# Local attention layers with a load semaphore each for the weights of queries and of keys

## The chip, the cores and the metric

The kernel runs on one core of one Trainium2 chip. The metric is the device time of one execution in microseconds (us), and the median of several runs stands for a kernel. PE is the tensor engine, DVE the vector engine, ACT the scalar engine, POOL GpSimd, and SP the engine whose queue issues the DMAs.

## The reference

Two blocks of gated cross attention and a feed-forward part, over an input of 32 sequences of 128 tokens with 128 features. The first "feed-forward" part is itself a stack of six local attention layers with an MLP each; nearly all of the time goes there, and the change touches nothing else.

```python
def attn_layer(x, Wqkv, qs, ksc, Wo):          # 16 heads of 64, windows of 32 tokens
    q, k, v = jnp.split(x @ Wqkv, 3, -1)       # each (b, heads, n, 64) after sh
    q = l2norm(q) * qs
    k = l2norm(k) * ksc
    q = q * cos * scale + rotate_half(q) * sin * scale
    k = k * cos * inv + rotate_half(k) * sin * inv
    out = local_attention(q, k, v)             # softmax over this window and the one before
    return out.transpose(0, 2, 1, 3).reshape(b, n, INNER) @ Wo

for i in range(6):
    x = attn_layer(shift_tokens(x), Wqkv[i], q_scale[i], k_scale[i], Wo[i]) + x
    x = ffn_layer(shift_tokens(x), ln_g[i], ln_b[i], W1[i], b1[i], W2[i], b2[i]) + x

x = x + jnp.tanh(g_xattn[0]) * cross_attention_0(layernorm(x), ctx)
x = x + jnp.tanh(g_ffn[0]) * local_layers(layernorm(x))
x = x + jnp.tanh(g_xattn[1]) * cross_attention_1(layernorm(x), ctx)
x = x + jnp.tanh(g_ffn[1]) * quantised_linear(layernorm(x))
```

## The kernel before

Activations stay in SBUF for the whole kernel. There are three phases: the first cross attention, `local_layers` with all six layers, and the second cross attention with the quantised linear. Between phases every engine drains.

In `local_layers` a unit u is one sequence of one layer, 6 x 32 = 192 units. Every engine runs the same loop over steps, and in a step it does a stage of several units at once: the projection of queries and keys of unit `step`, their transposes of unit `step - 1`, the scores of `step - 2`, the value projection of `step - 4`, the mix of `step - 6`, and the MLP of a group of four sequences between 7 and 13 steps behind. The order of the stages in a step is written out by hand for each engine; there is no scheduler. Engines wait for each other by semaphores with constant counts. The pipeline doesn't empty between layers: step 32 k is the first of a new layer, and in it PE still makes values, scores and MLP of the old one.

PE's order in a step is: queries (`project(step, 0)`), the MLP's third up projection (every fourth step, the first of a layer among them), `mix`, keys (`project(step, 1)`), values (`project(step - 4, 2)`), `scores`, the output projection (odd units), other parts of the MLP, and the transposes of keys and of queries. Each of these takes one of four pairs of PSUM banks in turn (`ROTATING`), and `banks.fill` waits for the reader of what the pair held four turns ago. At the first step of a layer the values take the pair of that step's queries, so PE waits there for `producted[0]`, which DVE raises on line 1027. The scores take the pair of the third up projection and wait for `hidden_made`, which DVE raises on line 1101.

Weights have one buffer each: queries, keys and values lie side by side in `w_qkv`, and the head scales `qs` and `ks` in `head_scales`. SP loads a part of the next layer when PE has made the last projection with it. In the last-but-one step of a layer, behind the copies of moved values (`place_v`), it issues the query weights and the query scales (`load_qk(sp, layer + 1, 0)`), and in the last step, behind the four DMAs that bring turned probabilities back (`place_probs`), the key weights and the key scales (`load_qk(sp, layer + 1, 1)`). Behind those stand the DMAs of `place_v` and the store of turned probabilities.

All four DMAs of a layer raise the common semaphore `qk_loaded`, which is at `QK * (layer + 1)` when the last has landed. Two waits use it: PE's before the first query projection of a layer, and DVE's in `start_layer`, which stands before all DVE's work of the step and makes `rot`, the rotary tables multiplied by the head scales. `start_layer` has four small products of two SBUF tiles (128x64 each): the two for queries on lines 1012 and 1014, then the two for keys on the same lines. Behind it DVE's order is: the query products with `rot` (lines 1026 and 1027, one operand in PSUM; they also wait for ACT's squares, line 896), the turning of probabilities (line 1074), the gelu product (line 1101), and the key products (lines 1026 and 1027 again).

ACT's order at the start of a step is: squares of the queries, the reciprocal norms of the unit before (line 907), one gelu, squares of the keys. POOL's is: rotation of the keys of the unit before (line 1154), their normalisation and that of its queries (both line 1162, which wait for line 907), subtraction of the row maxima (line 1140), rotation of the queries (line 1154), and normalisation of probabilities (line 1146). All POOL's operations have both inputs in SBUF.

Of the kernel before, what the change touches and what calls it, by code (L numbers as in the profile page):

```python
# [16 lines left out]
P = 128  # L17
NB, S, D = 32, 128, 128
# [9 lines left out]
INNER = H * HD  # L28
IT = INNER // P
FF = int(D * 4 * 2 / 3)  # L30
FTILES = [(o, min(P, FF - o)) for o in range(0, FF, P)]
# [33 lines left out]
def each(n):  # L65

    def of(stage):
        def run(u, *more):
            if 0 <= u < n:
                stage(u, *more)  # L70
        return run
    return of
# [46 lines left out]
def build(nc, dram):  # L119
    stack = ExitStack()  # L120
    with stack:
# [3 lines left out]
        def sem(name):  # L125
            return stack.enter_context(nc.semaphore(name))
# [426 lines left out]
        def local_layers(phase):  # L553
            here = ExitStack()
            with here:
# [28 lines left out]
                (gelu,) = ring("gelu", 1, [P, len(FTILES), GT])  # L584
                mlp_x2 = mlp_xs[:, :, :].rearrange("p b s -> p (b s)")

            qk_loaded, wv_loaded, wo_loaded, mlp_loaded = sem("qk_loaded"), sem("wv_loaded"), sem("wo_loaded"), sem("mlp_loaded")
            QK, WV, WO, MLP = 16 * 4, 16, 16, 16 * (1 + 3 * len(FTILES) + 3)
            zeroed, rot_made, xs_ready = sem("zeroed"), sem("rot_made"), sem("xs_ready")
            projected = [sem(f"projected_{k}") for k in "qkv"]  # L590
            v_copied, v_placed = sem("v_copied"), sem("v_placed")
# [1 line left out]
            squared, producted, summed, rotations, normalised, turned, copied = (  # L593
                [sem(f"{n}_{k}") for k in "qk"]
                for n in ("squared", "producted", "summed", "rotations", "normalised", "turned", "copied"))
# [17 lines left out]
            for step in range(UNITS + LAST):  # L613
                for stage, lag, every in ROTATING:
                    u = step - lag
# [9 lines left out]
            def load_qk(sp, layer, part):  # L625
                if layer:
                    sp.wait_ge(projected[part], NB * layer)
                sp.dma_start(w_qkv[:, part * INNER:(part + 1) * INNER],
                             dram["l_wqkv"][layer, :, part * INNER:(part + 1) * INNER]).then_inc(qk_loaded, 16)
                if layer:  # L630
                    sp.wait_ge(rot_made, 4 * layer)
                sp.dma_start(head_scales[:, part, :, :].rearrange("p s d -> p (s d)"),
                             dram[("l_qs", "l_ks")[part]][layer].partition_broadcast(P)).then_inc(qk_loaded, 16)

            def load_v(sp, layer):
                if layer:
# [54 lines left out]
            def load_first(sp):  # L691
                load_qk(sp, 0, 0)
                load_qk(sp, 0, 1)
                load_v(sp, 0)
                load_out(sp, 0)
                load_mlp(sp, 0)

            def sp(sp):
                for step in range(UNITS + LAST):
                    place_probs(step - 5, sp)  # L700
                    layer, into = step // NB, step % NB
                    if layer < DEPTH - 1 and into == NB - 1:
                        load_qk(sp, layer + 1, 1)
                    if 0 < layer < DEPTH and into == 3:
                        load_v(sp, layer)
                    place_v(step - 4, sp)
                    if layer < DEPTH - 1 and into == NB - 2:
                        load_qk(sp, layer + 1, 0)
                    if 0 < layer < DEPTH and into == 5:
                        load_out(sp, layer)  # L710
                    if 0 < layer < DEPTH and into == 12:
                        load_mlp(sp, layer)
                    store_probs(step - 4, sp)
                sp.wait_ge(probs_placed, P_PLACED * UNITS)

            def pe(pe):
# [3 lines left out]
                @each(UNITS)  # L720
                def project(u, part):
                    g = u // GB
                    i = pair_of["qkv"[part], u]
                    banks.fill(pe, i, (producted[part] if part < 2 else v_copied, u + 1))
                    if u % NB == 0 and part == 0:
                        pe.wait_ge(qk_loaded, QK * (u // NB + 1))
                    if u % NB == 0 and part == 2:
                        pe.wait_ge(wv_loaded, WV * (u // NB + 1))
                    if u % GB == 0 and part == 0:
                        pe.wait_ge(xs_ready, g + 1)  # L730
                    for j in range(2):
                        mm = pe.matmul(pairs[i][:, j * BANK:(j + 1) * BANK], xs[g % 2][:, u % GB, :],  # L732
                                       w_qkv[:, part * INNER + j * BANK:part * INNER + (j + 1) * BANK], start=True, stop=True)
                    mm.then_inc(projected[part], 1)
# [107 lines left out]
                for step in range(UNITS + LAST):  # L842
                    project(step, 0)
                    mlp_up(step - 13, 2)
                    mix(step - 6)
                    project(step, 1)
                    project(step - 4, 2)
                    scores(step - 2)
                    project_out(step - 6)
                    mlp_up(step - 11, 0)  # L850
                    mlp_mean(step - 7)
                    mlp_up(step - 11, 1)
                    mlp_variance(step - 10)
                    mlp_down(step - 13)
                    transpose_qk(step - 1, 1)
                    transpose_qk(step - 1, 0)
# [146 lines left out]
            def dve(dve):  # L1003
                phase_gate(dve, phase)

                def start_layer(layer):
                    dve.wait_ge(qk_loaded, QK * (layer + 1))
                    if layer:
                        dve.wait_ge(producted[0], NB * layer)
                        dve.wait_ge(producted[1], NB * layer)  # L1010
                    for i in range(2):
                        dve.tensor_tensor(rot[:, 2 * i, :, :], tables[:, 2 * i, :, :], head_scales[:, i, :, :],
                                          ALU.mult).then_inc(rot_made, 1)
                        dve.tensor_tensor(rot[:, 2 * i + 1, :, :], tables[:, 2 * i + 1, :, :], head_scales[:, i, ::-1, :],
                                          ALU.mult).then_inc(rot_made, 1)
# [96 lines left out]
                for step in range(UNITS + LAST):  # L1112
                    if step < UNITS and step % NB == 0:
                        start_layer(step // NB)
                    products(step, 0)
                    turn_probs(step - 5)
                    mlp_hidden(step - 13, 2)
                    products(step, 1)
                    mask_scores(step - 2)
                    sum_squares(step, 0)  # L1120
                    mlp_centre(step - 7)
                    add_out(step - 6)
                    mlp_hidden(step - 11, 0)
                    add_down(step - 13)
                    sum_squares(step, 1)
                    mlp_hidden(step - 11, 1)
                    row_sums(step - 4)
                    clamp_norms(step)
                    row_maxima(step - 2)
# [51 lines left out]
            return load_first, sp, pe, act, dve, pool  # L1181

        f0_load, f0_sp, f0_pe, f0_act, f0_dve, f0_pool = local_layers(1)

        def second_attention(phase):
# [714 lines left out]
```

## Time and profile before

| | |
|---|---|
| median of 3 runs | 3425.03 us (3424.27 to 3427.98) |
| the profiled execution's own time | 3413.21 us |
| its span | 3411.4 us |
| mean granted clock of PE | 0.982 of full speed |
| local layers in the span | from about 243 to 3060 us |
| busy over the span | PE 95%, DVE 86%, POOL 77%, ACT 70% |
| chain of work that ended last | PE 84%, issue 5%, POOL 4%, ACT 3%, DVE 3% |

The profile is of one execution, with times in us from the start of the span. A timeline row has the start, the time taken, engine, line of the kernel, operation and tiles, the count if equal operations are merged, and in brackets the idle time of the engine before it with what ended it. "issue" there means that nothing which the profile shows ended it; a wait for a semaphore that a DMA raised long before is not told apart from others by that. In the time that an operation took, what it stood still after its start is contained.

The page names the costliest groups: the projections on line 732 (1081.2 us busy on PE) are the first, POOL's rotations on line 1154 (908.7 us) the second. A step lasts some 14.5 us, so the 192 units take most of the span.

### The profile page before, as it was taken

The numbers are of one execution on the slowest core, as the hardware profiler recorded it, in microseconds if no ns is written. First come the engines' busy times: TensorE is split into PE (matmuls) and PEld (weight loads), VectorE is DVE, ScalarE is ACT, GpSimd is POOL, SyncE is SP. The second block draws the span as 40 slices with busy tenths as digits, with TensorE's granted clock in tenths as the row PEclk, the third lists the DMA queues.
The fourth block names the chain that finished last, engine by engine and source line by source line (L and its number), as shares of the span: only waits on it lengthen the run. The fifth ranks groups of instructions, "written<-read, shape, count | busy, mean of one in ns | idle before, by whom it ended". The sixth has DMA issues, their size and how long they took to land.

```text
span 3411.4 us, 130897 instructions
## 1 busy us (share of the span) xinstructions
PE 3245.9 (95%) x56355; PEld 2054.7 (60%) x56386; DVE 2943.4 (86%) x3343; ACT 2379.1 (70%) x4288; POOL 2639.8 (77%) x1408
## 2 busy tenths in 40 slices
PE   7977999999999999999999999999999999977996
PEld 4545666666666666666666666666666666643554
DVE  6869989889999999998989898898999999935887
ACT  6865677667676767676776776776767676746885
POOL 1229988888888888888888888888888888833576
PEclk9989999999999999999999999999999999988998
DMA  2002333443433344334433334343344333330000
GB/s 94 2 1 64 122 113 111 120 126 114 120 112 112 117 126 119 113 108 126 125 113 117 112 110 123 119 120 113 113 125 125 118 111 112 110 123 1 2 11 17
DMA packets 229188, 336.05 MB, mean 99 GB/s; under 512 B 39046, under 2 KB 151044, under 8 KB 228228
## 3 DMA queue, kind: packets, MB, share of 16 engines
q1 hardware_dynamic: 228612, 327.68, 31.7%
q8 instruction: 446, 7.31, 0.9%
q14 instruction: 130, 1.06, 0.1%
HBM read 124.14 MB, written 102.76 MB: 67 GB/s over the span
## 4 chain that ended last, share of the span: by engine, by line
PE 84%; issue 5%; POOL 4%; ACT 3%; DVE 3%; SPq 0%; DMA 0%; POOLq 0%; DVEq 0%; ACTq 0%
PE psum L732 29%; PE psum L800 10%; PE psum L742 9%; PE psum L786 8%; PE psum L759 8%; PE psum L827 7%; PE psum L838 4%; POOL f_rotated L1154 2%; ACT x_expo L1480 1%; PE psum L817 1%; PE psum L809 1%; ACT x_expo L391 1%; PE psum L1337 1%; PE psum L1347 1%; PE psum L309 1%
## 5 line engine op out<-in xcount | busy, mean ns | idle before, releaser
L732 PE MATMUL psum<-w_qkv,f_xs 128*128 128x512 f32 x2304 | 1081.2, 606 | 18.9 <-issue 14.2
L1154 POOL TENSOR_TENSOR f_rotated<-f_times_cos,f_times_sin 128x1024 f32<-128x1024 f32 x384 | 908.7, 2367 | 9.3 <-DVE f_times_sin L1027 9.3
L1162 POOL TENSOR_TENSOR f_rotated<-f_rotated,f_rnorm 128x1024 f32<-128x1024 f32 x384 | 722.6, 1903 | 38.2 <-ACT f_rnorm L907 11.9
L732 PEld LDWEIGHTS psum<-w_qkv,f_xs 128*128 128x128 f32 x2304 | 410.1, 191 | 402.4 <-issue 393.6
L896 ACT ACTIVATE f_squares<-psum 128x1024 f32<-128x1024 f32 x384 | 392.9, 1023 | 361.4 <-PE psum L732 356.4
L1146 POOL TENSOR_TENSOR f_probs<-f_probs,f_rowsum 128x1024 f32<-128x1024 f32 x192 | 365.2, 1902 | 329.1 <-DVE f_rowsum L1066 329.1
L1026 DVE TENSOR_TENSOR f_times_cos<-psum,rot 128x1024 f32<-128x1024 f32 x384 | 469.8, 1223 | 131.6 <-ACT f_squares L896 127.8
L914 ACT COPY f_qkT<-psum 128x1024 f32<-128x1024 f32 x384 | 369.9, 1013 | 210.8 <-PE psum L742 210.7
L1027 DVE TENSOR_TENSOR f_times_sin<-psum,rot 128x1024 f32<-128x1024 f32 x384 | 466.1, 1214 | 0.0
L1034 DVE TENSOR_REDUCE f_sumsq<-f_squares 128x16 f32<-128x1024 f32 x384 | 463.4, 1209 | 0.0
L742 PEld LDWEIGHTS psum<-consts,f_rotated 128*128 128x128 f32 x3072 | 348.5, 141 | 98.0 <-issue 89.2
L742 PE MATMUL psum<-consts,f_rotated 128*128 128x128 f32 x3072 | 371.1, 274 | 17.7 <-POOL f_rotated L1162 14.7
L1140 POOL TENSOR_TENSOR f_probs<-f_probs,f_negmax 128x1024 f32<-128x1024 f32 x192 | 365.2, 1902 | 0.0
L786 PEld LDWEIGHTS psum<-f_probsT,f_v 64*64 64x64 f32 x6144 | 262.9, 135 | 163.1 <-issue 163.1
L800 PE MATMUL psum<-f_outT,w_o 128*128 128x256 f32 x1536 | 358.6, 387 | 1.2 <-ACT f_outT L928 1.2
L759 PEld LDWEIGHTS psum<-f_qkT 64*32 64x32 f32 x24576 | 254.2, 105 | 146.9 <-issue 145.3
L786 PE MATMUL psum<-f_probsT,f_v 64*64 64x64 f32 (+1 forms) x6144 | 310.1, 228 | 15.8 <-issue 15.8
L800 PEld LDWEIGHTS psum<-f_outT,w_o 128*128 128x128 f32 x1536 | 285.1, 190 | 45.5 <-issue 1.8
L786 PE MATMUL psum<-f_probsT,f_v_moved 64*64 64x32 f32 (+1 forms) x12288 | 307.5, 217 | 0.0
L827 PE MATMUL psum<-f_xn,w 128*128 128x512 f32 (+1 forms) x576 | 281.2, 612 | 7.7 <-ACT f_xn L970 7.7
L759 PE MATMUL psum<-f_qkT 64*32 64x64 f32 x24576 | 285.4, 225 | 0.8 <-issue 0.8
L786 PEld LDWEIGHTS psum<-f_probsT,f_v_moved 64*64 64x64 f32 x12288 | 286.2, 136 | 0.0
(175 smaller groups left out, 5159.5 us busy)
## 6 DMA issues: line engine op xcount, KB each, us to landing
f_v_moved<-f_v SPq DMA_DIRECT2D x768, 128.0 KB, 2.8
turned_blocks<-w_qkv SPq DMA_DIRECT2D x192, 512.0 KB, 3.0
f_probsT<-turned_blocks SPq DMA_DIRECT2D x768, 128.0 KB, 2.8
w_qkv<-in_l_wqkv SPq DMA_DIRECT2D x18, 512.0 KB, 4.0
w_o<-in_l_wo SPq DMA_DIRECT2D x6, 512.0 KB, 4.6
w_qkv<-in_ctxT SPq DMA_DIRECT2D x1, 2048.0 KB, 8.7
out<-x_f_result SPq DMA_DIRECT2D x8, 256.0 KB, 2.2
w<-in_l_w SPq DMA_DIRECT2D x6, 341.0 KB
```

Of the source, the lines that this page charges most:

```text
L732: mm = pe.matmul(pairs[i][:, j * BANK:(j + 1) * BANK], xs[g % 2][:, u % GB, :], w_qkv[:, part * INNER + j * BANK:part * INNER + (j + 1) * ...
L742: tr = pe.transpose(pairs[i][:, t * S:(t + 1) * S], rotated[u % 2][:, part, 2 * t:2 * t + 2, :].rearrange("p h d -> p (h d)"), ident)
L759: mm = pe.matmul(pairs[i][these, at:at + NEAR], qkT[u % 2][rows, 0, t, these], qkT[u % 2][rows, 1, t, near], start=True, stop=True, tile_p ...
L786: mm = pe.matmul(pairs[i][cols, at + windows.start * WIN:at + windows.stop * WIN], values, probsT[u % 2][rows, windows, j, :], start=True, ...
L800: mm = pe.matmul(pairs[i][:, 0:GT // 2], w_o[:, t, :], outT[:, t, tokens], start=t == 0, stop=t == IT - 1)
L827: mm = pe.matmul(pairs[i][0:n, a * BANK:a * BANK + GT], w_1[:, a * FF + o:a * FF + o + n], xn[:, :], start=True, stop=True)
L896: act.activation(squares[part][:, :], pair("qk"[part], u), ACT.Square).then_inc(squared[part], 1)
L1026: dve.tensor_tensor(halves(times_cos[part][:, :]), halves(taken), table(0), ALU.mult)
L1027: dve.tensor_tensor(halves(times_sin[part][:, :]), halves(taken)[:, ::-1], table(1), ALU.mult).then_inc(producted[part], 1)
L1034: dve.tensor_reduce(sumsq[u % 2][:, part * H:(part + 1) * H], squares[part][:, :].rearrange("p (s h d) -> p h s d", s=2, h=H), axis=XY, op ...
L1154: pool.tensor_tensor(rotated[u % 2][:, part].rearrange("p h (s d) -> p s h d", s=2), halves(times_cos[part][:, :]), halves(times_sin[part] ...
L1162: pool.tensor_tensor(rt, rt, rnorm[u % 2][:, part * H:(part + 1) * H].unsqueeze(2).broadcast_to([P, H, HD]), ALU.mult).then_inc(normalised ...
```

## The change

The common semaphore is replaced by two, `q_loaded` and `k_loaded`, each raised by two DMAs per layer. PE waits for the first before its first query projection of a layer and for the second before its first key projection. In `start_layer` DVE waits for `q_loaded` and `producted[0]`, makes the two query products of `rot`, and then waits for `k_loaded` and `producted[1]` and makes those for keys. SP issues the same DMAs in the same order behind the same waits, and no instruction of PE, ACT, DVE or POOL is moved, added or left out, but for the waits.

```diff
-            qk_loaded, wv_loaded, wo_loaded, mlp_loaded = sem("qk_loaded"), sem("wv_loaded"), sem("wo_loaded"), sem("mlp_loaded")
-            QK, WV, WO, MLP = 16 * 4, 16, 16, 16 * (1 + 3 * len(FTILES) + 3)
+            q_and_k_loaded = [sem("q_loaded"), sem("k_loaded")]
+            wv_loaded, wo_loaded, mlp_loaded = sem("wv_loaded"), sem("wo_loaded"), sem("mlp_loaded")
+            QK, WV, WO, MLP = 16 * 2, 16, 16, 16 * (1 + 3 * len(FTILES) + 3)
...
                 sp.dma_start(w_qkv[:, part * INNER:(part + 1) * INNER],
-                             dram["l_wqkv"][layer, :, part * INNER:(part + 1) * INNER]).then_inc(qk_loaded, 16)
+                             dram["l_wqkv"][layer, :, part * INNER:(part + 1) * INNER]).then_inc(q_and_k_loaded[part], 16)
                 if layer:
                     sp.wait_ge(rot_made, 4 * layer)
                 sp.dma_start(head_scales[:, part, :, :].rearrange("p s d -> p (s d)"),
-                             dram[("l_qs", "l_ks")[part]][layer].partition_broadcast(P)).then_inc(qk_loaded, 16)
+                             dram[("l_qs", "l_ks")[part]][layer].partition_broadcast(P)).then_inc(q_and_k_loaded[part], 16)
...
                     banks.fill(pe, i, (producted[part] if part < 2 else v_copied, u + 1))
-                    if u % NB == 0 and part == 0:
-                        pe.wait_ge(qk_loaded, QK * (u // NB + 1))
+                    if u % NB == 0 and part < 2:
+                        pe.wait_ge(q_and_k_loaded[part], QK * (u // NB + 1))
...
                 def start_layer(layer):
-                    dve.wait_ge(qk_loaded, QK * (layer + 1))
-                    if layer:
-                        dve.wait_ge(producted[0], NB * layer)
-                        dve.wait_ge(producted[1], NB * layer)
                     for i in range(2):
+                        dve.wait_ge(q_and_k_loaded[i], QK * (layer + 1))
+                        if layer:
+                            dve.wait_ge(producted[i], NB * layer)
                         dve.tensor_tensor(rot[:, 2 * i, :, :], tables[:, 2 * i, :, :], head_scales[:, i, :, :],
                                           ALU.mult).then_inc(rot_made, 1)
```

## Rows read from the trace of the kernel before

**Rows 1.** The list of waits, PE: who waited for whom, us, times, longest us.
```profile
PE psum L732 <- issue: 14.2, 5, 3.3
```

**Rows 2.** Timeline of PE, start of the fourth layer: start us, us, engine, line, operation [idle before].
```profile
1597.04 1.91 PE L742 MATMUL psum<-consts,f_rotated 128*128 128x128 f32 x16
1601.91 3.00 PE L732 MATMUL psum<-w_qkv,f_xs 128*128 128x512 f32 x4 [2.96 <-issue]
...
1612.37 0.84 PE L759 MATMUL psum<-f_qkT 64*32 64x64 f32 x65
```

**Rows 3.** Timeline of SP's queue there: issues of the head scales of queries and of keys.
```profile
1587.40 0.43 SPq L632 DMA_DIRECT2D head_scales<-in_l_qs  x1
...
1596.98 0.43 SPq L632 DMA_DIRECT2D head_scales<-in_l_ks  x1
```

**Rows 4.** Timeline of DVE there: rot products, query products and a gelu product.
```profile
1601.85 0.42 DVE L1012 TENSOR_TENSOR rot<-consts,head_scales 128x64 f32<-128x64 f32 x1 [0.49 <-DMA head_scales<-in_l_ks]
1602.19 2.38 DVE L1014 TENSOR_TENSOR rot<-consts,head_scales 128x64 f32<-128x64 f32 x1
1604.49 0.21 DVE L1012 TENSOR_TENSOR rot<-consts,head_scales 128x64 f32<-128x64 f32 x1
1604.62 0.21 DVE L1014 TENSOR_TENSOR rot<-consts,head_scales 128x64 f32<-128x64 f32 x1
1606.01 1.23 DVE L1026 TENSOR_TENSOR f_times_cos<-psum,rot 128x1024 f32<-128x1024 f32 x1 [1.17 <-ACT f_squares L896]
...
1609.44 0.71 DVE L1101 SCALAR_TENSOR_TENSOR f_gelu<-psum,b,f_gelu 85x512 f32<-85x512 f32 x1
```

**Rows 5.** Timeline of PE at the starts of layers two, three, five and six.
```profile
670.23 1.91 PE L742 MATMUL psum<-consts,f_rotated 128*128 128x128 f32 x16
...
686.83 1.48 PE L759 MATMUL psum<-f_qkT 64*32 64x64 f32 x128
...
1134.99 1.91 PE L742 MATMUL psum<-consts,f_rotated 128*128 128x128 f32 x16
...
1148.97 1.49 PE L759 MATMUL psum<-f_qkT 64*32 64x64 f32 x128
...
2065.99 2.87 PE L732 MATMUL psum<-w_qkv,f_xs 128*128 128x512 f32 x4 [2.79 <-issue]
...
2524.52 1.91 PE L742 MATMUL psum<-consts,f_rotated 128*128 128x128 f32 x16
2528.64 1.96 PE L732 MATMUL psum<-w_qkv,f_xs 128*128 128x512 f32 x4 [2.21 <-issue]
2530.43 1.88 PE L827 MATMUL psum<-f_xn,w 128*85 128x512 f32 x4
...
2533.78 3.70 PE L732 MATMUL psum<-w_qkv,f_xs 128*128 128x512 f32 x8
2537.41 1.48 PE L759 MATMUL psum<-f_qkT 64*32 64x64 f32 x128
```

**Rows 6.** A window of rows 2's first projections: length, busy us by engine, PE's granted clock, DMA share, GB/s.
```profile
1602.70:1606.00 3.30, 3.30 (x5) 1.14 (x4) 2.13 (x3) 1.02 (x1) 1.78 (x1) 0.50 0.00 0
```

**Rows 7.** Timeline of POOL, start of the fourth layer.
```profile
1588.37 2.36 POOL L1154 TENSOR_TENSOR f_rotated<-f_times_cos,f_times_sin 128x1024 f32<-128x1024 f32 x1
1590.87 3.76 POOL L1162 TENSOR_TENSOR f_rotated<-f_rotated,f_rnorm 128x1024 f32<-128x1024 f32 x2
...
1600.28 1.90 POOL L1146 TENSOR_TENSOR f_probs<-f_probs,f_rowsum 128x1024 f32<-128x1024 f32 x1 [1.46 <-DVE f_rowsum L1066]
1602.14 2.34 POOL L1154 TENSOR_TENSOR f_rotated<-f_times_cos,f_times_sin 128x1024 f32<-128x1024 f32 x1
1606.57 3.76 POOL L1162 TENSOR_TENSOR f_rotated<-f_rotated,f_rnorm 128x1024 f32<-128x1024 f32 x2 [2.09 <-ACT f_rnorm L907]
```

**Rows 8.** Timeline of DVE and POOL in the second attention, a stretch of 2 us.
```profile
3201.80 1.99 DVE L1653 TENSOR_SCALAR x_f_cen<-x_f_cen,x_f_inv 128x128 f32<-128x128 f32 x1
3201.81 1.90 POOL L1710 TENSOR_TENSOR x_expo<-x_expo,x_total 128x1024 f32<-128x1024 f32 x1 [2.15 <-DVE x_total L1596]
```

## The prediction

> **What bounds the kernel now.** PE is busy for 95% of the span and makes up most of the page's chain of work that ended last, so I looked first for the places where PE stands still, in the list of waits. For the projections on line 732 it has one row of waits that no engine is named for: 14.2 us in 5 waits, the longest 3.3 [rows 1]. Five is the number of layer changes, and the timeline shows all five waits in one place, before the first query projection of a new layer. I take the fourth layer's start as the pattern [rows 2] and call the end of the last transposes T0 (1597.04 + 1.91 = 1598.95). PE then idles 2.96 us, projects queries (4 matmuls), runs the MLP's third up projection (4), the mix, keys and values (8), and reaches the scores at 1612.37, T0 + 13.42. The queue of SP says why it idles: the query scales were issued at 1587.40, long before T0, but the key scales only at 1596.98 [rows 3], and the common semaphore is full only when those have landed, up to 1601.85, where DVE's wait on them ends [rows 4].
>
> The same distance, T0 to the scores, is 686.83 - 672.14 = 14.69 at the start of the second layer, 1148.97 - 1136.90 = 12.07 at that of the third and 2537.41 - 2526.43 = 10.98 at that of the last [rows 5]. Without idle time the stretch is 10.98 - 2.21 = 8.77 long. The fifth layer's projections look like the fourth's (a wait of 2.79, then 2.87 against 3.00 for the four matmuls), and I count 8.77 + 2.79 + 1.7 = 13.26 for it. The sum of the five is 64.4, and 64.4 - 5 x 8.77 = 20.6 us lie over the least: 14.2 idle, and 6.4 in which the matmuls ran longer. That second part is the clock: in the fourth layer four projections took 3.00 us behind the wait, against 1.96 in the last layer, and while they ran the granted clock was 0.50 [rows 6], 1.2 GHz instead of 2.4; before the wait PE had been busy without a gap. By the stretches it costs 0 behind the waits of 3.3 and 2.21, 1.69 (13.42 - 8.77 - 2.96) in the fourth layer, 1.7 in the fifth, and 14.69 - 8.77 - 2.9 = 3.0 in the second, whose wait is what 14.2 leaves.
>
> **What the change does at each layer change, with times from T0.** No instruction moves or goes away. Layer 0 starts with everything loaded; nothing changes there.
>
> PE: query weights landed before T0, so the 2.96 go, and PE starts at T0: queries to 1.8, up to 3.6, mix to 5.15 (lengths from the last layer's start [rows 5], where the clock was full). The new wait for keys stands in front of the key projection; it holds back keys, values, scores and all behind, but it was filled by T0 + 2.9, so it costs nothing, and keys end at 6.97. The extra semaphore instruction on PE, six in all, is put at zero: its bound above is some hundredths of a us.
>
> The next thing late is DVE. The value projection uses the pair of banks that the query projection filled four turns earlier, so it waits for both query products of DVE (lines 1026 and 1027). These stand behind the four small rot products, and there is the difficulty. Rot products take 0.21 us [rows 4], but one here took 2.38, another 0.42, and each of the two ended 0.08 us after an operation of POOL: 1602.27 after 1602.18, 1604.57 after 1604.48 [rows 4, 7]. Read together: a DVE product with both inputs in SBUF stands still while POOL runs, gets in between two POOL operations, and only one of them does. The Trainium skill, "SBUF — State Buffer", section "SBUF: two separate sides", has this as an exclusive lock that the shared port pair grants to whichever started first, for the whole instruction; the trace agrees.
>
> Before the change the last two rot products, for keys, ran in 0.34 us, for POOL had nothing to do between 1604.48 and 1606.57: it waited for ACT's reciprocal norm, which stood behind ACT's square of the late query projection [rows 7]. That idle time disappears with the change. POOL starts 1606.57 - 1604.91 = 1.66 after PE's queries end; from T0 + 1.8 this makes T0 + 3.5, before its operation on line 1154 is through at T0 + 5.53. So POOL goes on to line 1162 at once: 0.14 behind, as 1590.87 stands behind 1588.37 + 2.36, at 5.67. The rot products for queries are unchanged, since both had been held by POOL and not by the keys (end 5.62). The first for keys starts at 1604.49, 0.13 before POOL, and gets in. The second would start at 5.67 and end its predecessor at 5.75: POOL is there first. How close a race DVE loses is seen in another phase: a DVE operation that started at 3201.80, POOL's at 3201.81, and DVE took 1.99, until POOL's end [rows 8]. So the second stands still for one POOL operation of 1.9 and ends at about 7.65.
>
> From there, by the distances of [rows 4]: query products from 7.8 (I allow 0.1 for the semaphore), two of 1.22, to 10.2; PE's values from there to 12.0; the gelu product (line 1101), which frees the scores' banks, ends 4.14 behind the products' start, 11.95. **The scores start at T0 + 12.0.** PE has meanwhile idled from 6.97 to 10.2, 3.2 us, so the wait has only moved behind the keys. Five times 12.0 is 60.0: 4.4 less than 64.4, before the clock.
>
> The clock: five waits of 3.2 instead of 2.94, 3.30, 2.96, 2.79 and 2.21. The four that are near to it cost 3.0, 0, 1.69 and 1.7, mean 1.6; five of them 8.0. Its bounds are 0 and 5 x 3.0. So the change is 60.0 + 8.0 - 64.4 = **+3.6 us**, from -4.4 to +10.6. Behind the scores I put nothing. DVE's key products follow the gelu product and so start as PE starts the scores; the transposes, which need their banks, come after the scores and the down projection. That DVE and POOL are no later there than PE can bear is an assumption.
>
> The profiled execution took 3413.21 (span 3411.4), the median of the runs 3425.03, 12 us more. What the 12 us are the rows don't tell; the sum is a difference between two profiled executions, 3413.2 to 3416.8, and I add it to the median: 3428.6.
>
> **Rivals.**
> A. *Both rot products for keys get in before POOL.* For it: the first is there 0.13 early, and the order of the last is a tie on the rows. Against it stands the lost race of [rows 8]. Query products at 5.9, values at 8.3, scores 10.25: five times that is 51.3, 13.1 less, and a wait of 1.3 leaves the clock alone. 3411.9. A chance of 0.22.
> B. *Slower: POOL gets in before each of the two*, so that both lines 1162 go first. It decides if the first key product asks later than 0.14 after the end of line 1154; the new wait for the keys' semaphore stands right in front of it and may put it off by that much. Products at 9.7, scores 13.9: 69.5, so +5.1, and five waits of 5 us, each dearer in clock than the 3.0 seen: up to +15. 3440, 3432 at least. A chance of 0.2.
> C. *The change does nothing*: PE's start would still wait if the query weights, too, landed late. They are issued 9.6 us ahead of the keys' in SP's queue [rows 3]; the chance is 0.03. Nor does the reading that the whole 20.6 us come back hold: the values need DVE's query products, and rot alone ends at 5.6.
> D. My forecast, 0.55.
>
> **Numbers.** A measurement of this kernel can tell about 0.2%, 6.85 us, from no change. D is within it but for its upper end (clock costs near 3 in most layers); A is faster; B is mostly slower. Faster 0.24, same 0.47, slower 0.29. The range has A, D and the lower part of B: 3410 to 3438; of D alone it would be 3420 to 3436.
>
> **What would show it.** In the profile after: PE's 732 row without its five waits at T0, and a wait of 3.2 before the 3rd group of projections (values) instead; the fourth rot product with some 1.9 us, the third with 0.2 to 0.3; POOL without idle time between 1154 and 1162; scores at T0 + 12.0 where the clock stays up. A is shown by two short key products and a wait of 1.3, B by two long ones. I am wrong outright if PE is held before the keys, or if products with one operand in PSUM also stand still for POOL.

## The result and the profile after

| | before | after |
|---|---|---|
| first series, median | 3424.65 us (3418.79 to 3427.98, 6 runs) | 3403.74 us (3399.82 to 3413.93, 6 runs) |
| profiled execution, own time | 3413.21 us | 3404.29 us |
| its span | 3411.4 us | 3402.5 us |

The ratio is 0.9944 with a 95% interval from 0.9927 to 0.996: the change makes the kernel faster by 0.4 to 0.7%, some 21 us by the medians of this series. I had forecast 3.6 us more and a range from 3410 to 3438; the measured median lies below it.

The wait list of PE after the change has for line 733 (732 before) no row with "issue" left. In its place stands this (who waited for whom: us in total, times, longest):

```profile
PE psum L733 <- DVE f_times_sin L1027: 7.6, 5, 1.5
```

It answers to [rows 1]: five waits, one per layer change, but 1.5 us each instead of 2.2 to 3.3, and for DVE's query products. The timeline of PE at the start of the fourth layer answers to [rows 2]:

```profile
1597.53 1.91 PE L743 MATMUL psum<-consts,f_rotated 128*128 128x128 f32 x16
1599.28 1.88 PE L733 MATMUL psum<-w_qkv,f_xs 128*128 128x512 f32 x4
1600.99 1.88 PE L828 MATMUL psum<-f_xn,w 128*85 128x512 f32 x4
...
1604.34 1.99 PE L733 MATMUL psum<-w_qkv,f_xs 128*128 128x512 f32 x4
1607.84 1.99 PE L733 MATMUL psum<-w_qkv,f_xs 128*128 128x512 f32 x4 [1.52 <-DVE f_times_sin L1027]
1609.76 1.49 PE L760 MATMUL psum<-f_qkT 64*32 64x64 f32 x128
```

T0, the end of the transposes, is 1599.44. The query projection follows at once, then the up projection, the mix and the keys; the values wait 1.52 us, and the scores start at T0 + 10.32. All five layer changes look the same: 10.31 or 10.32 us, 51.6 in all, against 64.4 before. DVE and POOL at the same place answer to [rows 4] and [rows 7]:

```profile
1601.77 0.99 DVE L1012 TENSOR_TENSOR rot<-consts,head_scales 128x64 f32<-128x64 f32 x1
1602.68 2.39 DVE L1014 TENSOR_TENSOR rot<-consts,head_scales 128x64 f32<-128x64 f32 x1
1604.99 0.21 DVE L1012 TENSOR_TENSOR rot<-consts,head_scales 128x64 f32<-128x64 f32 x1
1605.13 0.21 DVE L1014 TENSOR_TENSOR rot<-consts,head_scales 128x64 f32<-128x64 f32 x1
1605.43 1.23 DVE L1026 TENSOR_TENSOR f_times_cos<-psum,rot 128x1024 f32<-128x1024 f32 x1
```

```profile
1600.77 1.90 POOL L1146 TENSOR_TENSOR f_probs<-f_probs,f_rowsum 128x1024 f32<-128x1024 f32 x1 [1.45 <-DVE f_rowsum L1066]
1602.63 2.35 POOL L1154 TENSOR_TENSOR f_rotated<-f_times_cos,f_times_sin 128x1024 f32<-128x1024 f32 x1
1605.13 3.83 POOL L1162 TENSOR_TENSOR f_rotated<-f_rotated,f_rnorm 128x1024 f32<-128x1024 f32 x2
```

The idle time of POOL before line 1162 is gone, as forecast. But the fourth rot product took 0.21 us. It was to lose against line 1162, which starts in the same hundredth of a microsecond, 1605.13. Instead POOL's two operations took 3.83 together and not 3.76: POOL was the one that stood still, for 0.07 us. In nanoseconds the trace has the product's start 3 ahead of POOL's, and 1 to 5 ahead in all fifteen layer changes of the changed kernel's three profiles.

The granted clock of PE (the third number from the end; columns as in [rows 6]) was full in the whole stretch:

```profile
1599.50:1611.00 11.50, 9.98 (x238) 5.09 (x238) 11.38 (x14) 7.52 (x11) 10.08 (x6) 1.00 0.37 124
```

### The profile page after: what moved, and what is told of

The parts are those of the page before. It is cut to its first block and busy times, and to the rows that moved or that the text cites. A ratio compares the mean times of both kernels' runs of the same rounds, so it can differ in the third digit from the quotient of the medians.

```text
span 3402.5 us, 130907 instructions
## 1 busy us (share of the span) xinstructions
PE 3247.4 (95%) x56355; PEld 2059.5 (61%) x56386; DVE 2942.0 (86%) x3343; ACT 2379.8 (70%) x4288; POOL 2640.0 (78%) x1408
## 5 line engine op out<-in xcount | busy, mean ns | idle before, releaser
L787 PE MATMUL psum<-f_probsT,f_v 64*64 64x64 f32 (+1 forms) x6144 | 309.7, 228 | 15.6 <-issue 15.6
```

Source lines behind the costliest of these rows:

```text
L787: mm = pe.matmul(pairs[i][cols, at + windows.start * WIN:at + windows.stop * WIN], values, probsT[u % 2][rows, windows, j, :], start=True, ...
```

## The experiments

Each kernel was timed against the kernel before; its profile is one more execution. "Stretch" is the time from the end of the last transposes of a layer to the scores behind them, as in the prediction.

**How large is the gain, and how much does a profile differ from the next?** The kernel before and the changed kernel were run again, with no edit.

> The kernel before, unchanged, timed against itself. If the change's 20 us are all its own, this gives 0 within 0.1% and a profile like the first one. Rival: the profiled execution of before (3413.2 us, 11 us under its median) was an uncommonly quick one, so that part of the 20 us is what the tensor clock costs at the layer changes in other executions. Then this profile has a span some us longer, with the five stretches from the last transposes to the scores summing to more than 64.4 us (up to 75) or with more low clock in the attention phases.

Measured: 3416.37 us against 3418.97, ratio 0.9992 (0.998 to 1.0003). The stretches were 13.60, 12.97, 11.80, 13.05 and 13.24, together 64.7 (64.4 in the first profile). Its own time was again low, 3412.59, with nothing uncommon at the layer changes. So the first expectation held. This execution was itself the second quickest of twelve, so it doesn't show what the layer changes cost in slow ones. The profile of DVE's half alone (below), where PE also starts late, is of a slow one: its span is 3427.0, 16 us longer than the two of before, and its five stretches come to 65.7, only 1 us more. As far as one profile can tell, then, the rival falls too, and the spread between executions is elsewhere.

> The changed kernel, unchanged, timed against the kernel before in five rounds. Theory: the waits at the layer changes are worth 13 us plus what the low clock cost there, so 13 to 20 us less than before (ratio 0.994 to 0.996), and each of the five stretches from the last transposes to the scores is again 10.31 us, since it hangs on an order of operations and not on chance. Rival: the race between the last rot product and GpSimd, which was won in the profile by 2 ns, is won by chance; then one or more stretches of this profile are near 12.0.

Measured: 3408.17 us (10 runs) against 3418.97 (27), ratio 0.9966 (0.9954 to 0.9978); stretches 10.32 five times, the fourth rot product 0.21 us five times. The race was not won by chance: the order came out the same every time.

> The changed kernel once more against the kernel before, for the size of the gain: the two series gave ratios of 0.9944 and 0.9966. If only the stretches at the layer changes differ (13.0 us of 64.5, with the clock's cost in them), the ratio is 0.9962 and this series lies within 0.995 to 0.997; if there is a gain outside of them, it lies at 0.9944 again. Each stretch again 10.31 us, the fourth rot product again 0.21 us.

Measured: 3406.63 us (12 runs) against 3421.38 (23), ratio 0.996 (0.9946 to 0.9974), as for a gain in the stretches alone; stretches 10.31 five times. The three series give 0.9944, 0.9966 and 0.996; the last two have the more runs and name 10.8 and 14.8 us. The stretches alone, 64.4 or 64.7 less 51.6, are 13 us, a ratio of 0.9962, which lies in the last two intervals and 0.0002 outside the first. I take about 13 us as the effect, and the 21 of the first series as this and the spread between executions. The same can be seen in the profiles from the first and last start of the projections (line 732 or 733: shortest, middle and longest duration in ns, then first and last start), of before and of the changed kernel's three:

```profile
L732 PE MATMUL psum<-w_qkv,f_xs x2304: 589/592/1220, 244.9 to 3030.1; 128*128 128x512 f32 x192
```

```profile
L733 PE MATMUL psum<-w_qkv,f_xs x2304: 590/593/1221, 251.0 to 3021.2; 128*128 128x512 f32 x192
```

```profile
L733 PE MATMUL psum<-w_qkv,f_xs x2304: 592/592/1220, 251.0 to 3024.9; 128*128 128x512 f32 x192
```

```profile
L733 PE MATMUL psum<-w_qkv,f_xs x2304: 592/592/1220, 255.0 to 3030.2; 128*128 128x512 f32 x192
```

From first to last they need 2785.2 before and 2770.2, 2773.9 and 2775.2 after: 15, 11 and 10 us less. The first attention, which the change doesn't touch, ends 6 to 10 us later in the three profiles after than in the one of before. That isn't the change's doing: the projections start at 245.1 in the kernel with one more product, which has the whole change, and at 251.2 with DVE's half alone. It goes with PE's granted clock up to there: 0.97 in before, where they start at 244.9, 0.93 in the first profile after (251.0) and 0.91 in the third (255.0). Here lies a part of the spread between executions: the first and the third profile after differ by 9.2 us in span with equal stretches, and 4.0 of it are in this phase.

**Each half of the change alone.** First PE's: the waits of the changed kernel on PE, and both semaphores at once on DVE.

```diff
                 def start_layer(layer):
                     for i in range(2):
                         dve.wait_ge(q_and_k_loaded[i], QK * (layer + 1))
                         if layer:
                             dve.wait_ge(producted[i], NB * layer)
+                    for i in range(2):
                         dve.tensor_tensor(rot[:, 2 * i, :, :], ...
```

> PE's half of the change alone: PE waits for the queries' semaphore before its first query projection and for the keys' before the key projection; VectorE waits for both semaphores before its first rot product, as before the change. Theory (all of the gain is PE's start; the rot products for queries are held by GpSimd and not by the loads): stretches of 10.31 us as in the changed kernel and the same time within 0.1%. Rival (VectorE's half carries part of it): stretches longer than 10.6 us. If the rot products come 0.1 us later, the last one may lose its race with GpSimd; then stretches near 12.0 us and 8 us more in all.

Measured: 3417.97 us (12 runs) against 3418.97, ratio 0.9995 (0.9981 to 1.0009): no gain that can be told. The theory fell. The rival held in three of the five layer changes, and the clause on a lost race with it, but at 13.4 to 13.8 instead of 12.0, with a low clock behind the wait. The stretches were 13.60, 13.81, 13.37, 10.31 and 10.32, together 61.4, 3 us less than before. DVE and POOL at the third layer change:

```profile
1603.48 0.99 DVE L1013 TENSOR_TENSOR rot<-consts,head_scales 128x64 f32<-128x64 f32 x1 [2.23 <-DMA head_scales<-in_l_ks]
1604.39 0.21 DVE L1015 TENSOR_TENSOR rot<-consts,head_scales 128x64 f32<-128x64 f32 x1
1604.53 0.21 DVE L1013 TENSOR_TENSOR rot<-consts,head_scales 128x64 f32<-128x64 f32 x1
1604.66 1.92 DVE L1015 TENSOR_TENSOR rot<-consts,head_scales 128x64 f32<-128x64 f32 x1
```

```profile
1602.03 2.36 POOL L1155 TENSOR_TENSOR f_rotated<-f_times_cos,f_times_sin 128x1024 f32<-128x1024 f32 x1
1604.53 3.83 POOL L1163 TENSOR_TENSOR f_rotated<-f_rotated,f_rnorm 128x1024 f32<-128x1024 f32 x2
```

Since DVE waits for the key scales, its first product asks only at 1603.48, when POOL's rotation (started 1602.03) already runs. So none of the four gets in ahead of the rotation. Behind it POOL pauses 0.14 us, three of the four products get in, and the fourth starts 0.13 behind POOL's next operation and takes 1.92 us, until that ends. In the other two layer changes the key scales landed before the rotation started, one product got in ahead of it, and the other three made the pause. PE then waited 3.36 us for the query products:

```profile
1609.08 3.19 PE L733 MATMUL psum<-w_qkv,f_xs 128*128 128x512 f32 x4 [3.36 <-DVE f_times_sin L1028]
1612.20 1.80 PE L760 MATMUL psum<-f_qkT 64*32 64x64 f32 x128
```

Then DVE's half: both waits on PE before the first query projection, DVE as changed.

```diff
-                    if u % NB == 0 and part < 2:
-                        pe.wait_ge(q_and_k_loaded[part], QK * (u // NB + 1))
+                    if u % NB == 0 and part == 0:
+                        for i in (1, 0):
+                            pe.wait_ge(q_and_k_loaded[i], QK * (u // NB + 1))
```

> VectorE's half of the change alone: VectorE waits for the queries' semaphore, makes two rot products, then waits for the keys' and makes the other two; PE waits for both semaphores before its first query projection, as before the change. Theory: PE starts as late as before, ScalarE's squares and so GpSimd's operation on line 1162 too, and the stretches from the last transposes to the scores stay at 11.5 to 12.1 us plus the clock's cost (sum 60 to 68 us, before: 64.4 and 64.7); same time as before within 0.1%. So the half that does nothing alone is worth 2 us per stretch only together with PE's, where it lets the first product ask before GpSimd starts line 1154. Rival (VectorE's half is worth time by itself): sum under 58 us.

Measured: 3421.33 us (12 runs) against 3421.38, ratio 1.0007 (0.9994 to 1.0021); stretches 13.27, 14.37, 13.42, 11.64 and 12.97, together 65.7. The theory held. (The stretch of 14.37 has a wait of 4.21 on PE: the key scales landed at T0 + 4.12 there.) PE and POOL at the fourth layer change:

```profile
2074.03 1.96 PE L734 MATMUL psum<-w_qkv,f_xs 128*128 128x512 f32 x4 [2.88 <-issue]
```

```profile
2077.63 3.76 POOL L1163 TENSOR_TENSOR f_rotated<-f_rotated,f_rnorm 128x1024 f32<-128x1024 f32 x2 [0.95 <-ACT f_rnorm L909]
```

PE idles as before the change, and so does POOL before its normalisation, where the key products find the port free. Neither half is worth anything measurable by itself, though PE's alone has 3 us less in the stretches of its profile, and the two together are worth 13 us.

**What one lost race costs.** One more small product of two SBUF tiles behind the four, then two more. They write to a part of the constants that nobody reads any more.

```diff
+                    for _ in range(1):
+                        dve.tensor_tensor(spare, tables[:, 2, :, :], tables[:, 3, :, :], ALU.mult)
```

> The changed kernel with one more small product on VectorE behind the four rot products of each layer (same shape, two SBUF inputs, result not used). It would start 0.13 us after the fourth, when GpSimd's operation on line 1162 has started. Theory (one small product gets in between two GpSimd operations): it stands still for one GpSimd operation, takes about 1.9 us, and the stretch from the last transposes to the scores grows from 10.31 to 12.0 to 12.3 us; with the clock's cost behind a wait of 3.2 us the kernel is 8 to 20 us slower than the changed one. Rival (the product's own 0.13 us is all it costs): stretches of 10.45 us and no difference in time.

Measured: 3418.09 us (10 runs), ratio to before 1.0009 (0.9994 to 1.0023), 10 to 14 us slower than the changed kernel by the medians of different series. The stretches were 15.64, 12.89, 11.98, 13.02 and 13.12, together 66.7, 15 more than the changed kernel's. The one of 11.98, at full clock:

```profile
1606.65 0.21 DVE L1014 TENSOR_TENSOR rot<-consts,head_scales 128x64 f32<-128x64 f32 x1
1606.78 0.21 DVE L1016 TENSOR_TENSOR rot<-consts,head_scales 128x64 f32<-128x64 f32 x1
1606.92 1.92 DVE L1019 TENSOR_TENSOR consts<-consts 128x64 f32<-128x64 f32 x1
```

```profile
1604.28 2.36 POOL L1158 TENSOR_TENSOR f_rotated<-f_times_cos,f_times_sin 128x1024 f32<-128x1024 f32 x1
1606.79 3.83 POOL L1166 TENSOR_TENSOR f_rotated<-f_rotated,f_rnorm 128x1024 f32<-128x1024 f32 x2
```

The product that starts at 1606.78 wins against POOL's at 1606.79, the next, 0.14 later, stands still for 1.92. This is the case that I had forecast for the changed kernel, with one product fewer: the query products start 1.9 us later, PE waits 3.19, and the scores start at T0 + 11.98. A product of 0.13 us costs 1.67. In the first layer change, the one of 15.64, two products lost: DVE's clamp of the norms had itself stood still behind POOL, so that the rot products asked only when POOL's rotation ran:

```profile
673.69 1.84 DVE L1046 TENSOR_SCALAR f_sumsq<-f_sumsq 128x32 f32<-128x32 f32 x1 [0.18 <-issue]
...
676.58 1.32 DVE L1014 TENSOR_TENSOR rot<-consts,head_scales 128x64 f32<-128x64 f32 x1
```

> As the kernel with one more small product, but two more. Theory (each GpSimd operation lets one through): the fifth and the sixth take 1.9 us each, stretches of 13.8 to 14.2 us without the clock's cost, 18 us and more slower than the changed kernel. Rival (once VectorE has the port it keeps it for the products that stand ready): the sixth takes 0.2 us, stretches as with one more, near 12.2 us.

Measured: 3440.93 us (4 runs), ratio to before 1.0062 (1.0043 to 1.0082), 33 to 37 us slower than the changed kernel; 26 of that are in the stretches, and where the rest lies is not shown. Both products stood still:

```profile
1616.77 3.78 DVE L1019 TENSOR_TENSOR consts<-consts 128x64 f32<-128x64 f32 x2
```

```profile
1622.87 3.78 PE L733 MATMUL psum<-w_qkv,f_xs 128*128 128x512 f32 x4 [5.04 <-DVE f_times_sin L1031]
```

So POOL's operations that start back to back let one product through each, which is what the prediction said of them. The stretches are 15.63, 15.46, 15.63, 15.64 and 15.64, together 78.0. Without the clock they would be near 13.8 (the values would start at T0 + 11.9 and take 1.98); behind the waits of 5 us the four projections took 3.61 once and 3.78 four times instead of 1.99, and the granted clock in the 8 us around them was 0.59 on average:

```profile
1620.00:1628.00 8.00, 5.13 (x110) 2.60 (x114) 6.86 (x7) 1.30 (x2) 4.69 (x3) 0.59 0.18 72
```

**A version that beats both.** What is left of the wait is that DVE's query products come behind four rot products, two of which stand still for POOL. The rot products need only the head scales, and those can be loaded as soon as the layer's own rot is made.

```diff
+            def load_scales(sp, layer):
+                if layer:
+                    sp.wait_ge(rot_made, 4 * layer)
+                for part in range(2):
+                    sp.dma_start(head_scales[:, part, :, :]..., ...).then_inc(scales_loaded, 16)
...
+                    if layer < DEPTH - 1 and into == 16:
+                        load_scales(sp, layer + 1)
...
                     mlp_hidden(step - 11, 1)
+                    if step < UNITS - 1 and step % NB == NB - 1:
+                        start_layer(step // NB + 1)
                     row_sums(step - 4)
```

> A version that goes on from the change: the head scales of the next layer are loaded in step 16 of a layer under a semaphore of their own, and VectorE makes all four rot products of the next layer in the last step of the old one, before its row sums, where GpSimd is idle. The weights of queries and keys keep a semaphore each. If the query products of VectorE, late behind rot, are what is left of the wait at a layer change (1.5 us before the value projections), the stretch falls from 10.31 to 8.8 us and the kernel is 7.5 us faster than the changed one, 21 us and more faster than before (ratio 0.993 or less). Rival: what is left is ScalarE's squares or GpSimd; then the stretch stays above 9.5 us.

Measured: 3397.57 us (3391.96 to 3399.87, 6 runs) against 3418.97, ratio 0.9931 (0.9917 to 0.9945): the fastest of all, 9 us under the middle of the changed kernel's medians. The stretches are 8.53 five times. The four products no longer race: the first asks 0.1 us before POOL's rotation ends, and the others run in POOL's idle time behind it:

```profile
1601.10 0.22 DVE L1019 TENSOR_TENSOR rot<-consts,head_scales 128x64 f32<-128x64 f32 x1
1601.23 0.22 DVE L1021 TENSOR_TENSOR rot<-consts,head_scales 128x64 f32<-128x64 f32 x1
1601.36 0.22 DVE L1019 TENSOR_TENSOR rot<-consts,head_scales 128x64 f32<-128x64 f32 x1
1601.50 0.22 DVE L1021 TENSOR_TENSOR rot<-consts,head_scales 128x64 f32<-128x64 f32 x1
```

```profile
1598.85 2.36 POOL L1163 TENSOR_TENSOR f_rotated<-f_times_cos,f_times_sin 128x1024 f32<-128x1024 f32 x1
1603.21 1.90 POOL L1155 TENSOR_TENSOR f_probs<-f_probs,f_rowsum 128x1024 f32<-128x1024 f32 x1 [2.00 <-DVE f_rowsum L1073]
```

Keys and values go through PE without a wait between them:

```profile
1606.24 3.70 PE L740 MATMUL psum<-w_qkv,f_xs 128*128 128x512 f32 x8
```

## Why the prediction was wrong, point by point

- *What bounds the kernel at a layer change.* Right: PE waited for the key loads, and starts at T0 now. The new wait for keys before the key projection costs nothing: the mix and the keys follow each other in the profile after.
- *What is late next.* Right: the values wait for DVE's query products (the wait list names line 1027 five times). The reading that all of the idle time comes back would have given 8.8 us a stretch; that took another change (the version with early rot products, 8.53).
- *POOL's idle time disappears.* Right, to 0.02 us: line 1162 was to start at T0 + 5.67, and started at 5.69. The rot products for queries were to end at 5.62 and ended at 5.63.
- *"The second would start at 5.67 and end its predecessor at 5.75: POOL is there first."* **This step failed.** The fourth product won, in every layer change of all three profiles of the changed kernel, and in each of the 11 other cases of the experiments in which it started a few ns before POOL's operation; four times more it was the third that did, and won (PE's half alone, one more product). The step had two grounds, and neither held. The first was that POOL starts before the product's predecessor ends. In the profile after, the predecessor ended at 1605.20, 0.07 behind POOL's start, and the product had the port all the same. The second was [rows 8], where a DVE operation that started 0.01 us ahead of POOL's lost. That was another kind (TENSOR_SCALAR, where the rot products are TENSOR_TENSOR). How far ahead it starts isn't the reason: over all ten profiles this operation started 7 to 14 ns ahead of POOL's 60 times and lost each time, and the rot products started 1 to 5 ns ahead 30 times and won each time. Whether the kind is the reason, or what runs around it, wasn't tried. The tie could be seen in the rows of before and I had it as rival A, at 0.22. The more careful reading would have been that a row of another operation doesn't settle a tie, and to leave the two cases near each other.
- *The price of that race.* Right in size: 12.0 was forecast for the scores with one product lost, and the kernel with one more product has 11.98. The term is worth 12.0 - 10.3 = 1.7 us a stretch, 8.4 in all.
- *The clock.* 8.0 us were forecast for five waits of 3.2; the waits were 1.5 and cost nothing. In the sum, +3.6 - 8.4 - 8.0 = -12.8, and 51.6 - 64.4 is the same. So both wrong terms hang on the one lost race. As a price for waits of that length 1.6 us a wait was too high: the kernel with one more product has four waits of 3.2, which cost 0.9, 0, 1.0 and 1.1 (stretches of 12.89, 11.98, 13.02 and 13.12), 0.8 on average, and the three waits of 3.4 in PE's half alone cost some 1.2 to 1.7 (at full clock its scores would have been at about 12.15).
- *Rival A* is what happened: scores at 10.25 (10.31), a wait of 1.3 (1.5), -13.1 us (13). Of its two reasons, that the first key product is there 0.13 early and that the last is a tie, both held.
- *Rival B* did not, but its price was roughly right: scores at 13.9 without the clock (13.8 with two products lost), 15.6 with it. Its "3432 at least" doesn't come out of its own terms, 3425.0 + 5.1 = 3430.1.
- *The range.* Its lower end, 3410, lay 1.9 us under A's time, 3411.9, which was worked out on top of a median of three runs, 3425.03. Rival A happened, and yet the median of the first series, 3403.74, is 8 us below its time; the later medians are 3406.63 and 3408.17, and later series put before at 3416.4 to 3421.4. A range whose end is nearly a case's middle has no place for the spread of medians, here some 4 us to either side.
- *What I had not seen.* The prediction had DVE's half of the change at nothing ("the rot products for queries are unchanged"). In fact, it decides the race, as it lets one product ask before POOL's rotation starts whenever the key scales land late.

## What to carry to other kernels

When a wait is removed, look at what else used the idle time that it made: here small DVE products had run in the idle time of POOL, and without it they had to fit into pauses of 0.14 us. Small operations that share a port with a long one are better moved to a place where the other engine is idle than made to race, since being 0.13 us late costs a whole operation of the other engine. And test the halves of a change together as well as alone: two edits that measure 0 each were 13 us together.

## What the runs showed of the hardware

- A DVE product with two SBUF inputs that asks while POOL runs stands still until POOL's operation ends, and the profile has that time in its duration: 0.99, 2.39 and 1.92 us for products of 0.21. The other way POOL's operation stood still for 0.07 us (3.83 instead of 3.76 for two). The exclusive lock of the Trainium skill ("SBUF — State Buffer", "SBUF: two separate sides") fits all of this. That whichever starts first gets the port, as the Trainium skill says there, fits the 30 near ties of the rot products; by the recorded starts it doesn't fit [rows 8], where the operation that started 0.01 us earlier took 1.99 us.
- Between two POOL operations that start back to back one product gets in (with two more products, both took 1.9 us), and in the pause of 0.14 us between lines 1154 and 1162, three do. A rot product that started 1 to 5 ns ahead of POOL's operation won each time, 30 of 30; one that started 0.13 us later lost each time, 13 of 13.
- Four projections behind a wait of 3.4 us took 3.19 us, and behind one of 5.0 us 3.78, instead of 1.99: the granted clock was 0.61 of full speed while the first four ran and 0.50, its lower level of 1.2 GHz, from 1623 to 1626 us for the second. After waits of 1.5 us, 17 in these profiles, the projections were never slow; after waits from 2.2 to 3.4 us, 21 of them, they were in 16; after waits from 4.2 to 5.1, seven, in all. The matmuls ahead of the waits had been running without a gap.
- The loads of the key scales landed late enough to hold DVE up to 2.23 us with PE's half alone, and at most 0.8 us before the change. From issue to landing they took over 5.0 us in 11 of 30 layer changes where PE starts early, and in 1 of 15 where it starts late. Why, and whether PE's earlier start has a part in it, stays open.
